# Exponentials moved forward in ScalarE's order, and reciprocals spread from four DRAM copies

## The reference

```python
qh = (q @ Wq + bq).reshape(Bn, Tq, H, DK)
kh = (k @ Wk + bk).reshape(Bn, Tk, H, DK)
vh = (v @ Wv + bv).reshape(Bn, Tk, H, DK)
attn = jnp.einsum('bqhd,bkhd->hbqk', qh, kh) * mask[None]
attn = attn - jnp.max(attn)                 # one maximum over everything
attn = jnp.exp(attn) * mask[None]
attn = attn / (jnp.sum(attn, axis=-1, keepdims=True) + 1e-15)
out = jnp.einsum('hbqk,bkhd->bqhd', attn, vh).reshape(Bn, Tq, H * DK)
x = out @ Wo + bo + residual
mu = jnp.mean(x, axis=-1, keepdims=True)
var = jnp.mean((x - mu) ** 2, axis=-1, keepdims=True)
return (x - mu) / jnp.sqrt(var + 1e-05) * gamma + beta
```

## Time and profile before

| | before |
|---|---|
| median of three runs | 1738.48 us |
| the profiled execution | 1738.39 us |
| its span, first to last instruction | 1736.5 us |
| PE busy | 1619.3 us (93%) |
| DVE busy | 1151.8 us (66%) |
| ACT busy | 935.5 us (54%) |
| POOL busy | 544.1 us (31%) |
| DMA moved | 382.11 MB, mean 220 GB/s |
| granted TensorE clock, mean | 0.982 |

### The profile page before, as it was taken

The page is one execution under the profiler, slowest core; times in us unless marked ns, Lnnn a source line. Parts: engine busy times, 40 slices in busy tenths (PEclk is TensorE's granted clock), DMA queues, the critical chain, the costliest instruction groups (busy, mean ns, idle before and its releaser), DMA issues. The chain is left out here.

```text
span 1736.5 us, 30465 instructions
## 1 busy us (share of the span) xinstructions
PE 1619.3 (93%) x10501; PEld 796.7 (46%) x10501; DVE 1151.8 (66%) x2138; ACT 935.5 (54%) x1383; POOL 544.1 (31%) x778
## 2 busy tenths in 40 slices
PE   4999999999999999999983999999999999999997
PEld 4445555455554555545531344444444444444443
DVE  6666555565556655566542777878778787878774
ACT  6755555555555555555534555555555555555542
POOL 0000000000000000000000567677666767677677
PEclk8999999999999999999995999999999999999999
DMA  6463444534445444453327999999999999999971
GB/s 231 146 226 121 164 176 151 222 122 160 172 157 217 127 154 172 163 211 128 153 97 247 265 308 314 290 286 292 313 318 295 291 313 316 278 293 297 310 234 73
DMA packets 92556, 382.11 MB, mean 220 GB/s; under 512 B 7520, under 2 KB 12768, under 8 KB 74592
## 3 DMA queue, kind: packets, MB, share of 16 engines
q1 hardware_dynamic: 92512, 381.53, 65.7%
HBM read 250.43 MB, written 131.07 MB: 220 GB/s over the span
## 5 line engine op out<-in xcount | busy, mean ns | idle before, releaser
L78 PE MATMUL ps_o<-u,p_hi 128*128 128x512 f16 x1024 | 389.7, 381 | 5.0 <-DVE p_lo L985 5.0
L69 PE MATMUL ps_s<-x_hi,g_hi 128*128 128x512 f16 x1024 | 389.1, 380 | 3.7 <-ACT s L496 3.7
L79 PE MATMUL ps_o<-u,p_hi 128*128 128x512 f16 x1024 | 389.4, 380 | 0.0
L80 PE MATMUL ps_o<-u,p_lo 128*128 128x512 f16 x1024 | 389.2, 380 | 0.0
L71 PE MATMUL ps_s<-x_hi,g_lo 128*128 128x512 f16 x1024 | 388.8, 380 | 0.0
L70 PE MATMUL ps_s<-x_lo,g_hi 128*128 128x512 f16 x1024 | 388.6, 380 | 0.0
L496 ACT ACTIVATE s<-ps_s,c_bias 128x512 f32<-128x512 f32 x256 | 176.1, 688 | 314.1 <-PE ps_s L71 311.0
L1052 POOL MEMSET zeros<- 128x256 f32 x1 | 0.3, 311 | 905.9 <-POOLq L138 905.9
L985 DVE TENSOR_TENSOR p_lo<-ps_p,p_hi 128x512 f16<-128x512 f32 x256 | 175.4, 685 | 126.3 <-ACT p_hi L902 126.0
L616 DVE TENSOR_TENSOR score_max<-score_max,tile_max 128x1 f32<-128x1 f32 x257 | 40.7, 158 | 310.5 <-ACT s L496 308.8
L912 ACT ACTIVATE y<-y,shift,rstd 128x512 f32<-128x512 f32 x128 | 104.1, 813 | 243.4 <-POOL shift L1073 238.9
(11 more groups left out here) (90 smaller groups left out, 2363.1 us busy)
## 6 DMA issues: line engine op xcount, KB each, us to landing
r_bc<-reciprocals SPq DMA_DIRECT2D x128, 512.0 KB, 8.1
scores<-s SPq DMA_DIRECT2D x30, 2048.0 KB, 7.6
x<-xT_in SPq DMA_DIRECT2D x32, 1024.0 KB, 9.5
u_halves<-u_out SPq DMA_DIRECT2D x64, 512.0 KB, 3.2
s_more<-scores SPq DMA_DIRECT2D x16, 2048.0 KB, 16.3
u<-u_halves SPq DMA_DIRECT2D x16, 2048.0 KB, 22.3
y<-x_in SPq DMA_DIRECT2D x32, 1024.0 KB, 18.1
out<-y SPq DMA_DIRECT2D x31, 1024.0 KB, 12.3
```

Source lines behind the costliest of these rows:

```text
L69: pe.matmul(out, lhs_hi, rhs_hi, start=first, stop=False)
L78: pe.matmul(out, lhs_hi, rhs_hi, start=False, stop=False, skip_group_check=True)
L79: pe.matmul(out, lhs_hi, rhs_lo, start=False, stop=False, skip_group_check=True)
L80: return pe.matmul(out, lhs_lo, rhs_hi, start=False, stop=False, skip_group_check=True)
```

## The change

Three edits. First, `reciprocals` in DRAM gets a dimension of four copies. The matrix of the sums has its columns repeated, so that all 32 partitions of a block hold sums (each value four times), and each of the four stores carries 32 partitions (32 KB) instead of 8. Second, a spread is sixteen DMAs of 16 partitions (128 KB each), each from a copy of its own in turn, instead of four DMAs of 64 partitions. Third, ACT's order in a unit: `norm` 2 and 3 move behind into the next unit, `fill` 3 too, and both `exps` stand in front of the unit's own `norm` calls.

```diff
+COPIES = 4
-    r_d = nc.dram_tensor("reciprocals", (UNITS, 2, NP, TT), F32, kind="Internal").ap()
+    r_d = nc.dram_tensor("reciprocals", (UNITS, COPIES, 2, NP, TT), F32, kind="Internal").ap()
...
-                    sp.dma_start(r_d[u % UNITS, :, 4 * a:4 * a + 4, th * HT:(th + 1) * HT],
-                                 r32[32 * q:32 * q + NP, u % 2, :]).then_inc(r_stored, 16)
+                    sp.dma_start(r_d[u % UNITS, :, :, 4 * a:4 * a + 4, th * HT:(th + 1) * HT],
+                                 r32[32 * q:32 * q + COPIES * NP, u % 2, :]).then_inc(r_stored, 16)
...
-                        rows = r_d[u % UNITS, h:h + 1, 4 * k:4 * k + 4, :].rearrange("a p t -> a (p t)")
-                        sp.dma_start(r_bc[rows_of(h), u % 2, 4 * k:4 * k + 4, :].rearrange("r p t -> r (p t)"),
-                                     rows.to_broadcast([NK, 4 * TT])).then_inc(bc_in[u % 2][k], 16)
+                        for c in range(COPIES):
+                            rows = r_d[u % UNITS, c, h:h + 1, 4 * k:4 * k + 4, :].rearrange("a p t -> a (p t)")
+                            to = slice(h * NK + c * NK // COPIES, h * NK + (c + 1) * NK // COPIES)
+                            sp.dma_start(r_bc[to, u % 2, 4 * k:4 * k + 4, :].rearrange("r p t -> r (p t)"),
+                                         rows.to_broadcast([NK // COPIES, 4 * TT])).then_inc(bc_in[u % 2][k], 16)
...
-            def group(g, last):
+            def group(g, first, last):
...
-                    halves(0, 1)
+                    behind = lambda t: None if first and u == 0 else norm(g if u else g - 1, (u - 1) % UNITS, t)
                     if more3:
                         tiny(n + 3)
+                    halves(0)
+                    fill(n, 3)
+                    halves(1)
+                    if more3:
                         exps(n + 3, u + 3, 0)
-                    halves(2, 3)
+                    behind(2)
+                    halves(2)
+                    if more3:
+                        exps(n + 3, u + 3, 1)
+                    halves(3)
+                    behind(3)
                     if more:
                         fill(n + 1, 0)
+                    halves(4, 5)
                     norm(g, u, 0)
-                    if more3:
-                        exps(n + 3, u + 3, 1)
-                    halves(4, 5)
                     if more:
                         fill(n + 1, 1)
+                    halves(6, 7)
                     norm(g, u, 1)
-                    halves(6, 7)
                     if more:
                         fill(n + 1, 2)
-                    norm(g, u, 2)
-                    if more:
-                        fill(n + 1, 3)
-                    norm(g, u, 3)
+                if last:
+                    norm(g, UNITS - 1, 2)
+                    norm(g, UNITS - 1, 3)
...
-                    dve.wait_ge(bc_in[s][p // 4], 16 * n - 16 * s + 32)
+                    dve.wait_ge(bc_in[s][p // 4], COPIES * (16 * n - 16 * s + 32))
...
-            sel_sum[h * NK:(h + 1) * NK, p % 4, 4 * h + p % 4] = 1.0 / P_SCALE
+            sel_sum[h * NK:(h + 1) * NK, p % 4, 4 * h + p % 4::NP] = 1.0 / P_SCALE
```

More of the change, by code:

```diff
@@ L949, in _ @@
             act.wait_ge(affine_in, 48)
-            for t in range(TB):
+            for t in range(TB - 1):
                 fill(0, t)
@@ L956, in _ @@
                 round_p(0, 0, p)
-            with act.Fori(0, NG - 1) as g:
-                group(g, False)
-            group(NG - 1, True)
+            group(0, True, False)
+            with act.Fori(1, NG - 1) as g:
+                group(g, False, False)
+            group(NG - 1, False, True)
         @block.vector
```

## The result

The changed kernel takes 1931.86 us (1930.1 to 1934.83, four runs) against 1738.57 in the same comparison: ratio 1.1115, interval 1.1097 to 1.1132. It is 193 us slower. The forecast was 58.

A forecast was written before the change was run, and what follows sets the result against it. The prediction took the DMA cycle of store, spread and loads (24.45 us a unit) and compute (24.37) as joint limits; 36 for spreads, 20 for stores and 2 for the end made +58: 1796 us, 8-in-10 range 1732 to 1885.

The forecast's parts named there:

- What bounds the kernel: Output phase: DMA side at 24.45 us a unit and compute at 24.37 bind together; freeing PE alone gives next to nothing.
- the ring: Output phase, DMA side: store of reciprocals, spread, loads, store again; 24.45 us a unit, which no engine can shorten.
- PE's wait: At each unit's sums PE waits 1.47 us for the second exponential; 28 units would give 41 us.
- ACT's order: ACT in the output phase: earlier exponentials soon wait for scores; phase end costs +2 us (bounds -3 to +5).
- The sixteen DMAs: Spread of reciprocals: issue at 0.60 us each sets its length, data rate stays near today's; +1.2 us a spread.
- slow bound: Spread data: 19.2 us at half of 218 GB/s, as a quarter of the partitions is written at a time.
- price of an issue: SP issuing a spread's DMAs: 0.60 us each, 9.6 us for sixteen (bounds 5.8 to 10.2).
- The stores: Reciprocal stores of 32 partitions instead of 8, directly ahead of the spread: +0.7 us a unit (bounds 0 and 1.5).
- The sum: Whole kernel: 36 us for thirty spreads, 20 for 29 stores, 2 for the end; 58 us slower, 1796 us.
- Rival 1 in part: Spread: DMA engines partly in step over few partitions, 140 to 150 GB/s, 14 us a spread; 1895 us; chance 0.14.
- the signs that I had named for the forecast: Mid-phase: spreads every 26.3 us at 190 to 220 GB/s, early PE waits gone, ACT awaiting scores, DMA share 0.93 or more.
- The second ring: SP's store of y waits for `norm` 3; chain about 22 us, under 24, costed at nothing; uncovered, up to 2 us.

The follow-up runs named there:

- a spread at 384 GB/s: Changed kernel with one 8 KB row of x spread to all 128 partitions in two DMAs, one-copy stores: 1702.10 us; with ACT's old order 1736.82.
- two queues: Loads of scores, x and u issued by ACT: 1746.10 us with new order and old spread, 1748.67 on the kernel before, 1903.92 on the changed kernel.
- 1912.47: Changed kernel with one copy of the reciprocals: sixteen DMAs of 16 partitions, stores of 8 partitions, new ACT order; 1912.47 us, ratio 1.1001.
- the move: SP's store of y moved behind the loads: changed kernel 1928.62 us, old spread with new order 1748.85, partitions 32 to 95 with new order 1731.52.
- the best version: Against the kernel before: new ACT order, eight copies, partitions 32 to 95 in one DMA, store of y behind the loads; 1731.52 us, ratio 0.9956.

## Why the prediction was wrong

Side and place were right; one term was far too small, and it carried the result.

- **What bounds the kernel.** Right. The order alone gave no gain (1744.69), and a spread at 384 GB/s gave 1702.10 with it and 1736.82 without: the ring and PE's wait were both there, each hiding the other. The picture of the ring was too narrow, though: I made it of the line in SP's queue, and two queues changed nothing for the spread of before. It also left a row out. I wrote that SP waits almost never for compute beyond the stores; the view of the earlier trace rows has this line too:

```profile
SPq L748 <- DVE r L971: 192.7, 25, 10.7
```

So SP waited for DVE's reciprocals in each unit. Where the trace was read this did not hold the ring: in the earlier trace rows that wait ends at 1220.49, with DMAs draining until 1232.

- **ACT's order.** I took +2 for the end of the phase. The first exponential of the last unit that has any stands at 1834.89 in the changed kernel, 94.0 us before the end; before, it was 91.6, so 2.4. Against the version with the same spread and the old order (89.8) it is 4.1. In all the order cost 5.5 us alone and 9.2 in the changed kernel. The rest of that was lost ahead of the last exponentials, for which I had no term: with the order alone that exponential stands at 1648.94, 4.0 us later than before.
- **The sixteen DMAs.** This step failed: "I take the value near today's, because DMAs to partitions 0 to 15, 16 to 31 and on queue behind each other in each DMA engine and those need not walk in step." The rate did not stay near today's: it fell from 213 to 131 GB/s, and a spread took 15.6 us, not about 11. 1912.47 - 1744.69 = 168 us over 30 spreads is +5.6 each, not +1.2. My slow bound, in full step over a quarter of the partitions, was 109 GB/s, so the DMA engines keep step for the larger part and not wholly. I had the mask loads' 215 GB/s, read them rightly as the target's limit, and then did not apply it once more. The price of an issue was off too (0.46, not 0.60), without effect. Nor does the working give the 1.2: a last DMA that begins at 10.2 and takes 0.6 to 1.2 us ends at 10.8 to 11.4, and with 0.4 for the finishing that is +0.4 to +1.0 on today's 10.8.
- **The stores.** +20 forecast, 1931.86 - 1912.47 = 19 measured. The table puts it outside the spread, at 0.5 us a unit, against the 0.7 that I took.
- **The sum.** 5.5 + 168 + 19 = 193, the steps from version to version, so it must add up. With 5.6 for 1.2 the forecast would have been 190 above.
- **Rival 1 in part** (14 us, 140 to 150 GB/s, 1895) was what came, somewhat worse: 131 GB/s and some 16 us. I gave it 0.14, and the range ended at 1885. Of the signs that I had named for the forecast only the DMA share came (0.96 of two units); the spreads came every 30.95 us instead of 26.3, and PE's wait at the sums grew instead of going.
- **The second ring** over the store of y, costed at nothing: about right for the changed kernel (SP waited for POOL 4.0 us in 600; the move gave 3 us), and in its cost for the old spread too, where the wait came in nearly every unit (91.9 us) and its removal gave nothing. It was wrong for a shorter spread (45.2 us; 15 us).

By the Trainium skill's page "SBUF — State Buffer" (Door 1: The DMA port swizzle), sixteen neighbours reach four ports, 0 to 63 and 0 to 31 the same eight, and 32 to 95, worked out from its port table, all sixteen. The runs agree in order: 131, 220 and 348 to 384 GB/s. The page's 104 GB/s for sixteen partitions is lower than the 131 here, where each DMA is followed at once by one to other partitions. That page was the best evidence at hand, and I left it a rival.

Open stays what holds the best version at 24.3 us a unit instead of 22.9. Its stores of reciprocals are eight times those of before (256 KB a unit). In the three versions with such stores and the new order the rest of the unit is 1.1 to 1.4 us longer than with the order alone, so they are a candidate, but they were not tried apart. Open is also why every second spread of partitions 32 to 95 and its neighbours is longer than the other.

## What to carry to other kernels

When a rate halves with half the partitions written, ask which partitions, and price the next halving before believing that queued DMAs even it out. Let a DMA write partitions from both halves or from far apart, in few large DMAs, and look at the rate, since 128 partitions from sixteen rows gave only 232 GB/s; more copies of the source did not pay here, since their stores cost as much as they gave, or more. A wait that an engine shows is worth nothing while another ring has the same period: here the order was worth 35 us, but only with a faster spread. And give the length of a spread as a mean over many units: with 32 to 95 in one DMA single spreads took 7.4 to 11.6 us, and the mean was 8.55.

## What the runs showed of the hardware that was not expected

The price of an issue on SP differed with its shape: 0.60 us for 64 partitions, 0.46 for sixteen neighbours, 0.63 for every fourth. And PE's clock fell after its waits: it had waited 1.78 and then 2.01 us for the two exponentials, the granted clock went from 1.00 up to 1308 to 0.50 from 1309 to 1315, and behind the sums PE started its products 0.43 us apart instead of 0.2155, at the lower of its two levels:

```profile
1310.02 1.94 PE L845 MATMUL ps_sum<-s_more,sel_sum 128*32 128x256 f32 x16 [2.01 <-ACT s_more L894]
1311.89 0.61 PE L79 MATMUL ps_o<-u,p_hi 128*128 128x512 f16 x1
1312.29 0.63 PE L80 MATMUL ps_o<-u,p_hi 128*128 128x512 f16 x1
1312.71 0.63 PE L81 MATMUL ps_o<-u,p_lo 128*128 128x512 f16 x1
```

The mean granted clock went from 0.982 to 0.929. What of the 193 us this makes was not separated. The DMA engines were busy for 0.95 of 1000 to 1600 us, and PE waits for exponentials in each unit, so most of it should be hidden.
